# Exponentials four pieces nearer to their maxima, maxima handed over by halves, and distance transforms one quarter later in an eight-batch attention and feed-forward kernel

## The reference

```python
x = x + attn_a(ln(x))   # values V = ln(x) wv; positions pos = ln(x) w3d + b3d, 3 per token
                        # dist = sqrt(sum((pos_i - pos_j)^2)); attn = softmax(-dist/4, causal); attn V wo + bo
x = x + ffn(ln(x))      # sigmoid(xr Wr) * (relu(xk Wk)^2 Wv), with xr, xk mixed from a token and the one before
x = x + attn_b(ln(x))   # 16 heads of 16: softmax(q k / 4, causal) v
x = x + ffn(ln(x))
```

## Time and profile before

| | |
|---|---|
| median of 3 runs | 2104.01 us (2102.3 to 2108.9) |
| profiled execution, device time | 2109.85 us |
| its span, first to last instruction | 2108.1 us |
| mean granted TensorE clock | 0.943 |
| busy: PE, DVE, ACT, POOL | 1849.2, 1467.0, 1323.7, 728.2 us |

### The profile page before, as it was taken

One profiled execution on the slowest core, in us unless ns is written; L12 is line 12 of the kernel. 1 busy time (PEld: TensorE's weight loads), 2 busy tenths in 40 slices (PEclk: granted clock), 3 DMA queues, 4 the chain that ended last, 5 costly groups with the idle time before them and its releaser, 6 DMA issues. The chain is left out here.

```text
span 2108.1 us, 32379 instructions
## 1 busy us (share of the span) xinstructions
PE 1849.2 (88%) x9842; PEld 922.5 (44%) x9842; DVE 1467.0 (70%) x4288; ACT 1323.7 (63%) x2585; POOL 728.2 (35%) x879
## 2 busy tenths in 40 slices
PE   5677898889997999889998899979998899988986
PEld 4453443335543455434543355434544345322423
DVE  5576778767676677667786667766776677768642
ACT  3564355876569565776758665695657766455664
POOL 1342332234333253333443243333532334312313
PEclk8797899999998999999999899989999999989998
DMA  3006113111131112410132111311124101322000
GB/s 85 1 23 123 26 56 67 31 31 32 55 76 31 31 31 82 80 21 12 41 110 42 31 31 56 76 31 31 34 83 76 22 11 41 99 33 50 13 21 20
DMA packets 64346, 97.26 MB, mean 46 GB/s; under 512 B 15655, under 2 KB 58029, under 8 KB 58030
## 3 DMA queue, kind: packets, MB, share of 16 engines
q1 hardware_dynamic: 64174, 95.20, 20.2%
HBM read 61.09 MB, written 33.55 MB: 45 GB/s over the span
## 5 line engine op out<-in xcount | busy, mean ns | idle before, releaser
L973 ACT ACTIVATE pt<-exp_bank 128x512 f32<-128x512 f32 (+1 forms) x1216 | 698.9, 582 | 526.6 <-PE exp_bank L935 521.0
L989 DVE CUSTOM_DVE_ANT_0 max_bank<-max_bank,mask 128x128 f32<-128x128 f32 (+3 forms) x1024 | 501.8, 500 | 400.9 <-PE max_bank L922 386.4
L922 PE MATMUL max_bank<-ks,qs 96*128 96x512 bf16 (+3 forms) x1536 | 523.5, 346 | 85.9 <-DVE piece_max L992 44.9
L935 PE MATMUL exp_bank<-qs,ks 98*128 98x512 bf16 (+3 forms) x1536 | 515.4, 342 | 40.0 <-ACT pt L973 37.0
L992 DVE TENSOR_REDUCE piece_max<-max_bank 128x1 f32<-128x512 f32 x512 | 344.1, 686 | 94.4 <-PE max_bank L922 90.2
L954 PE MATMUL o_bank<-pt,v 128*17 128x512 f32 (+3 forms) x3072 | 334.1, 508 | 13.7 <-POOL pt L1011 11.0
L922 PEld LDWEIGHTS max_bank<-ks,qs 96*128 96x128 bf16 x1536 | 150.9, 99 | 399.5 <-DVE piece_max L989 140.9
L1011 POOL TENSOR_SCALAR_AFFINE_SELECT pt<-pt 128x512 f32<-128x512 f32 x256 | 171.5, 670 | 412.6 <-ACT pt L973 411.8
L935 PEld LDWEIGHTS exp_bank<-qs,ks 98*128 98x128 bf16 x1536 | 152.4, 100 | 236.0 <-ACT pt L973 118.5
L633 PE MATMUL side<-vp,p 128*128 128x260 f32 x576 | 171.4, 423 | 28.7 <-ACT p L560 21.0
L412 ACT ACTIVATE xh<-xs,shift,rstd 128x256 f32<-128x256 f32 x256 | 149.7, 596 | 47.8 <-POOL shift L401 47.8
(11 more groups left out here) (119 smaller groups left out, 2348.4 us busy)
## 6 DMA issues: line engine op xcount, KB each, us to landing
parts_dram<-parts SPq DMA_DIRECT2D x64, 384.0 KB, 2.6
qs<-parts_dram SPq DMA_DIRECT2D x192, 128.0 KB, 7.2
ks<-parts_dram SPq DMA_DIRECT2D x32, 384.0 KB, 4.7
xs<-in_L_attn_a_x_dram SPq DMA_DIRECT2D x16, 512.0 KB, 4.2
ks<-parts_dram SPq DMA_DIRECT2D x32, 256.0 KB, 5.4
out_dram<-xs SPq DMA_DIRECT2D x16, 512.0 KB, 3.1
ks<-parts_dram SPq DMA_DIRECT2D x32, 128.0 KB, 5.8
qs<-neg_maxT SPq DMA_DIRECT2D x64, 8.0 KB, 1.9
```

Source lines behind the costliest of these rows:

```text
L922: pe.matmul(max_bank[u % MAX_BANKS][:, 0:k1 - k0], qs[r][0:KROWS, j, P * tile:P * (tile + 1)], ks[r][0:KROWS, j, k0:k1], start=True, stop= ...
L935: mm = pe.matmul(exp_bank[k % EXP_BANKS][:, (q1 - q0) * slot:(q1 - q0) * (slot + 1)], ks[r][:, j, P * kt:P * (kt + 1)], qs[r][:, j, q0:q1] ...
L973: act.activation(pt[:, e % 2, j + 1 - heads:j + 1, 0:w], exp_bank[k % EXP_BANKS][:, 0:heads * w].rearrange("p (j n) -> p j n", j=heads), A ...
L989: dve.tensor_tensor_reduce(scores, scores, mask[:, HALF - w:HALF], 1.0, LOWEST, ALU.add, ALU.max, piece_max[:, j, m:m + 1]).then_inc(max_f ...
```

## The change

- `LEAD` goes from 14 to 10: the exponential product in a quarter belongs to the piece ten before the maxima piece. Outputs and the last batch's `ffn4` move with it.
- The maxima are handed over by halves: the first after the group's fourth piece, the second after its twelfth. Each half has its own two small DVE operations, two turns on PE and a copy; SP sends it with eight transfers (two parts, four heads) of 1 KB, each from four rows of `neg_maxT` into a piece of one row of `qs`. PE waits for the first half at the group's first exponential product and for the second at that of its fifth piece.
- In `att1`, ACT's Ln, root and Exp, POOL's selects and PE's products come one quarter later. In batch 0 ACT's two squares of a piece come in its first two quarters. In batch 1 the third square moves from DVE to ACT.
- The rows of ones are filled by POOL, early in the setup (behind its second layer-norm shift), instead of by DVE.

```diff
-LEAD = NP + 2
+LEAD = NP - TPH + 2
...
-        "attend": [("attend", t, PIECE_AT[attended_from(t)] + 2, t // 2 + 1, 1, 2) for t in range(NT)],
+        "attend": [("attend", t, PIECE_AT[attended_from(t)] + 3, t // 2 + 1, 1, 2) for t in range(NT)],
...
-    rows = [(4 * NP * (g + 1) + 1, ("maxima", g)) for g in range(GROUPS)]
+    rows = [(4 * (NP * g + (NP if h else TPH)) + 1, ("maxima", g, h)) for g in range(GROUPS) for h in range(2)]
...
             for p in range(NP + 1):
+                for k in range(2 if n == 0 and p < NP else 0):
+                    yield at(PIECE_AT[p] + k)
+                    square(p, k)
                 for k in range(3):
-                    if p < NP and (k < 2 or n > 1):
+                    if p < NP and n > 0:
                         yield at(PIECE_AT[p] + PIECE_TIME[p] * 2 * k // 6)
                         square(p, k)
                     if p > 0:
-                        yield at(PIECE_AT[p] + PIECE_TIME[p] * (2 * k + 1) // 6)
+                        yield at(PIECE_AT[p] + PIECE_TIME[p] * (2 * k + 1) // 6 + 1)
                         transform(p - 1, k)
...
                 if p >= 2 and DIAGONAL[p - 2]:
-                    yield at(PIECE_AT[p])
+                    yield at(PIECE_AT[p] + 1)
                     select(p - 2)
...
-                    pe.wait_ge(crow_ready, 32 * (g + 1))
+                    pe.wait_ge(crow_ready, 256 * g + 128)
+                if m == TPH and j == 0:
+                    pe.wait_ge(crow_ready, 256 * g + 256)
...
-                if m == NP - 1 and j == GH - 1:
+                if m in (TPH - 1, NP - 1) and j == GH - 1:
+                    h = 0 if m < TPH else 1
+                    half = piece_max[:, :, TPH * h:TPH * (h + 1)]
                     dve.wait_ge(max_free, u + 1)
...
+                    if h == 1:
+                        dve.tensor_tensor(half, half, piece_max[:, :, NT:NP], ALU.max).then_inc(c_step, 1)
+                        dve.wait_ge(c_step, 3 * g + 2)
+                    dve.tensor_scalar(neg_max[:, h, 0, :, :], half, -1.0, None, ALU.mult).then_inc(c_step, 1)
+                    dve.wait_ge(c_step, 3 * g + 1 + 2 * h)
+                    dve.scalar_tensor_tensor(out=neg_max[:, h, 1, :, :], in0=half, scalar=-1.0,
+                                             in1=neg_max[:, h, 0, :, :], op0=ALU.mult,
                                              op1=ALU.subtract).then_inc(negmax_ready, 1)
...
-        def sp_maxima(g):
-            yield EMPTIED_AT["maxima", g] + 1
+        def sp_maxima(g, h):
+            yield EMPTIED_AT["maxima", g, h] + 1
             r = g % STACKS
-            nc.sync.wait_ge(negmaxT_ready, g + 1)
+            nc.sync.wait_ge(negmaxT_ready, 2 * g + h + 1)
             for c in range(2):
-                nc.sync.dma_start(qs[r][KROWS + c:KROWS + c + 1, :, :], neg_maxT[:, c, :]
-                                  ).then_inc(crow_ready, 16)
+                for j in range(GH):
+                    nc.sync.dma_start(qs[r][KROWS + c:KROWS + c + 1, j, HALF * h:HALF * (h + 1)],
+                                      neg_maxT[TPH * j:TPH * (j + 1), h, c, :]).then_inc(crow_ready, 16)
...
-            for r in range(STACKS):
-                yield SETUP_AT[7] + 12 + 8 * r
-                dve.memset(ks[r][KROWS:SROWS, :, :], 1.0).then_inc(rows_of_ones, 1)
...
             pool = nc.gpsimd
             yield SETUP_AT[6] + 6
+            pool.wait_ge(shift_ready, 2)
+            for r in range(STACKS):
+                pool.memset(ks[r][KROWS:SROWS, :, :], 1.0).then_inc(rows_of_ones, 1)
+            pool.wait_ge(rows_of_ones, STACKS)
             pool.memset(vp[:, :, ONE:ONE + 1], 1.0).then_inc(consts_ready, 1)
...
-                body = {"att1": [dve_att1(at, n)] + ([dve_squares(at, n)] if n < 2 else []), "proj3": [dve_proj3(at, n), dve_values3(at, n)]}.get(s, []) if h == 0 else []
+                body = {"att1": [dve_att1(at, n)] + ([dve_squares(at, n)] if n == 0 else []), "proj3": [dve_proj3(at, n), dve_values3(at, n)]}.get(s, []) if h == 0 else []
```

More of the change, by code:

```diff
@@ L273, in bass_hybrid @@
         piece_max = sb("piece_max", [P, GH, NP])
-        neg_max = sb("neg_max", [P, 2, GH, NT], BF16)
-        neg_maxT = sb("neg_maxT", [GH * NT, 2, P], BF16)
+        neg_max = sb("neg_max", [P, 2, 2, GH, TPH], BF16)
+        neg_maxT = sb("neg_maxT", [GH * TPH, 2, 2, P], BF16)
         pt = sb("pt", [P, 2, GH, HALF])
@@ L984, in dve_att3 @@
                 if m == 0 and j == 0 and g > 0:
-                    dve.wait_ge(negmax_ready, g)
+                    dve.wait_ge(negmax_ready, 2 * g)
                 scores = max_bank[u % MAX_BANKS][:, 0:w]
@@ L1024, in sp_att3, with pe_maxima @@
                         sp_load(n + X_BUFFERS, h)
[L1027 to L1030, removed]
+        def pe_maxima(g, h):
+            yield PARTS_AT["maxima", g, h][0]
+            nc.tensor.wait_ge(negmax_ready, 2 * g + h + 1)
+            bank = side_job(("maxima", g, h), negmaxT_ready, 2 * g + h + 1)[:, :].bitcast(BF16)
             for c in range(2):
-                mm = nc.tensor.transpose(bank[0:GH * NT, P * c:P * (c + 1)],
-                                         neg_max[:, c, :, :].rearrange("p j t -> p (j t)"), identb[:, :])
+                mm = nc.tensor.transpose(bank[0:GH * TPH, P * c:P * (c + 1)],
+                                         neg_max[:, h, c, :, :].rearrange("p j t -> p (j t)"), identb[:, :])
@@ L1034, in pe_maxima, with dve_maxima @@
             mm.then_inc(negmaxT_full, 1)
-        def dve_maxima(g):
-            yield EMPTIED_AT["maxima", g]
-            nc.vector.wait_ge(negmaxT_full, g + 1)
+        def dve_maxima(g, h):
+            yield EMPTIED_AT["maxima", g, h]
+            nc.vector.wait_ge(negmaxT_full, 2 * g + h + 1)
             if g > 0:
[L1040 to L1043, removed]
+                nc.vector.wait_ge(crow_ready, 256 * (g - 1) + 128 * (h + 1))
+            bank = side_of("maxima", g, h)[:, :].bitcast(BF16)
+            nc.vector.tensor_copy(neg_maxT[:, h, :, :],
+                                  bank[0:GH * TPH, 0:2 * P].rearrange("p (c n) -> p c n", c=2)
@@ L1207, in schedule @@
         def schedule(setup, attention, maxima, output, stage):
-            parts = list(setup) + [maxima(g) for g in range(GROUPS) if maxima]
+            parts = list(setup) + [maxima(g, h) for g in range(GROUPS) for h in range(2) if maxima]
             parts += [output(g, h) for g in range(GROUPS) for h in range(2) if output]
```

## The result

The kernel after takes 2166.0 us (median of 4 runs, 2162.0 to 2168.0), the kernel before 2106.5 (median of 4, 2102.3 to 2110.0): a ratio of 1.028, interval 1.0254 to 1.0308. It is 2.8% slower, where 2092 was forecast and the range ended at 2118. The profiled execution of after has a span of 2164.9 us against 2108.1, so +56.8 to explain.

What follows compares the result with a forecast made beforehand. PE was taken to bound most of a batch, ACT the stretch with distance work, DVE or the bank hand-over where no side job is due. Terms summed to -12.4 us: 2097.5 profiled, 2092 on the median's scale; range 2070 to 2118.

Steps and rivals of the forecast that it cites:

- sixteen small transfers a group: Maxima hand-over through SP: steady groups covered, seven short groups 0.9 to 2.5 us late; +12, up to about +41.
- the time left is as before: Second half's hand-over: still eight quarters after the group's end; copy to first exponential 6.17 us steady, 2.81 at shortest.
- The end: Last group: its first four exponential pieces run beside the last maxima, so everything after comes earlier; -9.9 us.
- Front start of exps: First group: four pieces of exponentials move into maxima pieces 10 to 13, where PE is busy; +4 (0 to +7).
- New partners: Across groups: wide exponentials fall beside wide maxima, saving time without side jobs and where PE idles; -16 (0 to -30).
- Rival 2: No change overall: new partners gain nothing and half maxima cost what they cost; 2108 us, chance 0.15.
- Maxima by halves: Every group: extra turns on PE, a copy and small operations on DVE, hidden where ACT limits; +17 (0 to +35).
- Ones on POOL: Front: without DVE's three fills, ACT's waits for distances shrink, less delay to DVE's copies; -5.5 (0 to -9.5).
- rival 4: Setup: each fill on POOL holds DVE's copies until it ends, so the front gains nothing; 2097 us, chance 0.08.
- Squares: First two batches' distances: earlier squares on ACT -3, third square moved from DVE to ACT -3; together -6 us.
- A quarter later: Attention's logs, roots, exps, selects and products: ACT waits less, and so PE behind POOL; -8 (-20 to +5).
- Rival 1: Maxima transfers: an issue step of 0.75 us makes short and most steady groups late; 2121 us, chance 0.17.

Runs made afterwards that it cites:

- b1_after_four: The kernel after with each half's maxima sent by four transfers of both rows instead of eight; 2110.7 us, ratio 1.0030.
- b2_halves_four: The kernel before with only the maxima by halves and distance 10, four transfers a half; 2109.4 us, ratio 1.0034.
- c2_eight_second: The kernel after with four transfers for the first half's maxima, eight kept for the second; 2165.4 us, ratio 1.0327.
- a1_halves: The kernel before with only the maxima by halves, distance 10 and eight transfers a half; 2142.1 us, ratio 1.023.
- f1_before_lead13: The kernel before with exponentials 13 pieces behind instead of 14, maxima whole, two transfers a group; 2187.2 us, ratio 1.0407.
- c3_lead12_four: The kernel before with only the maxima by halves, four transfers a half, exponentials 12 pieces behind; 2157.1 us, ratio 1.0298.
- e1: The kernel after with distance 11 instead of 10, eight transfers a half kept; 2101.5 us, ratio 0.9964.
- e2: The kernel after with distance 11 and four transfers a half; 2097.9 us, ratio 0.9973.
- d1_lead14_four: The kernel before with only the maxima by halves, four transfers a half, exponentials still 14 pieces behind; 2117.8 us, ratio 1.0090.
- a3_ones: The kernel before with only the three fills of ones moved from DVE to POOL; 2112.2 us, ratio 1.0043.
- a4_squares: The kernel before with only the squares changed: first batch's two earlier on ACT, second batch's third on ACT; 2113.2 us, ratio 1.0040.
- b4_no_quarter: The kernel after without the quarter's delay of logs, roots, exps, selects and products; 2143.8 us, ratio 1.0188.
- a2_quarter: The kernel before with only logs, roots, exps, selects and their products a quarter later; 2115.0 us, ratio 1.0103.
- e3: The kernel before with maxima by halves, distance 11, four transfers a half and the changed squares; 2088.5 us, ratio 0.9905.

## Why the prediction was wrong, step by step

**The failed step is the sixteen small transfers a group, +12 (up to +41), and in them "the time left is as before".** Their real price was 53 us (the kernel after against b1_after_four). That PE would wait at the second half was right; the issue step and the room were mis-sized, the parts' stores behind the issues and the price of a wait beyond its own length were put at nothing.

- *The issue.* 0.62 us a step, not 0.45. The row of three-row transfers (0.39) was the wrong neighbour; the median of the maxima's own (0.59) was the right one, which the rival had as the argument against itself. Time needed from the end of the copy: 5.97 us with eight transfers, 3.69 with four. This alone would not have put the forecast wrong: with 0.62 in the prediction's own sum the seven short groups are 7 x 1.19 us later and the six with a room of 6.17 us are 0.37 late, so the term is +23 and the forecast 2103.
- *The room.* The prediction took the shortest room of the kernel before's steady groups, 6.17 us from the copy's start, and kept it. But the room changed, and most in other groups. The exponentials of groups 7, 11, 15, 19 and 23 had 7.4 to 7.7 us in the kernel before. At a distance of 10 (b2_halves_four, where nothing waits there) they have 5.0 to 6.1, as other pieces stand between. With the quarter's delay as well (b1_after_four) they have 4.7 to 4.9. Group 19 in the three, copy and first product that uses it:

```profile
1372.81 0.27 DVE L1042 COPY neg_maxT<-side 32x256 bf16<-32x256 bf16 x1
...
1380.52 0.63 PE L935 MATMUL exp_bank<-qs,ks 98*128 98x512 bf16 x1
```

```profile
1384.92 0.21 DVE L1044 COPY neg_maxT<-side 32x128 bf16<-32x128 bf16 x1
...
1391.03 0.63 PE L937 MATMUL exp_bank<-qs,ks 98*128 98x512 bf16 x1
```

```profile
1389.50 0.21 DVE L1047 COPY neg_maxT<-side 32x128 bf16<-32x128 bf16 x1
...
1394.19 0.63 PE L940 MATMUL exp_bank<-qs,ks 98*128 98x512 bf16 x1
```

  Hence waits of 1.1 to 1.6 us before the exponentials of just these groups in the kernel after (they run beside the next group's maxima, so in the windows these waits stand in groups 8, 12, 16, 20 and 24), 9.4 us in all with groups 5, 9 and 25, and 18.8 in eight short groups in place of 14.5 in seven. The prediction priced the delay and the transfers apart; beside each other they cost more.
- *The queue behind the issues.* The prediction had "the batch's stores and part stores keep their places" and no price for it. Their place is behind the eight issues (5.2 us with gaps at group 14, where the two transfers of the kernel before took 1.5), DVE waits for the store, and 14.3 us of the 51.8 between c2_eight_second and b1_after_four stand in the groups where it does.
- *The price of a wait.* This was missing. Between c2_eight_second and b1_after_four, with equal instruction counts on every engine, the waits of PE differ by 27.1 us and the span by 51.8: PE's busy time is 23.2 us longer (1875.5 against 1852.3). The mean granted clock is 0.933 against 0.945: (1 - 0.933) x 2164.2 = 145 us of full clock not granted against (1 - 0.945) x 2112.4 = 116, 29 more. Without the groups where DVE waits, 37.5 us of span came with 27.1 of waits, 1.4 for one; between a1_halves and b2_halves_four it is 17.1 / 16.2 = 1.1, in f1_before_lead13 against the kernel before 75.6 / 53.7 = 1.4, and from group 28 on 20.1 / 12.1 = 1.7. That the waits bring the clock down is argued from the two coming together, from group 28 on above all, and not shown by itself: the clock also falls where nothing waits (mean 0.930 in c3_lead12_four; 0.87 and 0.90 in groups 3 and 4 of b2_halves_four, 1.00 in both in the kernel before).

The Trainium skill's advice to coalesce small transfers (DMA: Bandwidth & Descriptors, Rules for kernel authors), which the prediction set against this part and then priced low, was the right one: halving their number took 53 us off the kernel after. It was worth that much because the room was short: at a distance of 11 the same sixteen cost nothing that can be measured (e1 against e2: 2101.5 and 2097.9 us, ratios 0.9964 and 0.9973).

The other terms:

- *The end, -9.9:* right as a mechanism, -7.8 in b1_after_four. In the kernel after 3.3 us of wait and a clock of 0.75 took all but 1.3 of it.
- *Front start of exps, +4:* group 0 is 1.9 us longer in the kernel after, 3.3 in a1_halves. Right.
- *New partners, -16:* failed. The distances 14 and 10 with four transfers take 1356.1 and 1354.4 us in groups 5 to 26. Rival 2's first half was true. The gain was to be had at 11 (-22 against 10), which was found by trying it and not by this argument, and 12 costs +34. The like-with-like argument of the earlier trace rows fits 11 against 12, but does not rank 14; side jobs fall on other pieces with each distance, and what each share is stays open.
- *Maxima by halves, +17:* right in number, not in place, so in part luck. d1_lead14_four, which has the halves and neither long issues nor new partners, has a ratio of 1.009, that is 19 us. But a price of 0.55 a group makes 12 us in groups 5 to 26, and there its profile has 1.4 more than the kernel before (1356.1 against 1354.7); of 11.1 us in all 4.7 stand in groups 0 to 4.
- *Ones on POOL, -5.5:* failed by rival 4. a3_ones gives +1 to +17. The prediction had the rule of the Trainium skill (SBUF — State Buffer, Who interferes with whom) as a rival at 0.08, for want of a row of a fill; this trace now has it, four DVE operations held for 2.2 to 3.6 us. The rival's reckoning came true: the squares start 8.0 us late in a3_ones, and the three fills that no longer stand among the distances give just that back by the twelfth piece.
- *Squares, -6:* near in the front (group 0 begins 4.3 us earlier in a4_squares, and 1.5 in b4_no_quarter, which has the ones on POOL too), unclear at the end: ratio 1.004 alone, 2093.0 to 2088.5 us at a distance of 11, measured on two chips.
- *A quarter later, -8:* failed. a2_quarter loses 1.03%. PE's wait for POOL shrank as expected, but the time ahead of group 5 grew by 9.3 us (453.4 against 444.1), 7.0 of them in group 4 at the lower clock. Beside late transfers the delay cost about 20 us (b4_no_quarter), where it also took up to 1.4 us of the room and raised PE's waits for the maxima from 17.7 to 28.2 us.

Of what was to show it: the fills ended before 37 us and the waits of L550 in 30 to 60 us are down from 10.3 to 1.9, both as written, and yet the front gained nothing: the start had moved, and the delay held the rest. The eight issues take 4.9 us and not 3.2 to 3.6. The two signs of being wrong both came: waits in steady groups, and batches 1.1 to 6.1 us longer from group 8 to 24 (group 8 to 12 takes 248.9 us in place of 245.9).

Rival 1 came true in kind, but its price (2121) and its threshold (0.68 us a step) were both wrong. By the prediction's own rows the groups with a room of 6.17 us are late from (6.17 - 0.30 - 1.9) / 7 = 0.57 on; 0.62 was enough, the more as the room became smaller. And the loss of 59.5 us was more than three times the 17 by which 2121 lies above the 2104 before.

## What to carry to other kernels

When a hand-over is moved, measure the room in the new order and not in the old one: the pieces that lie between release and use change with the distance, a delay that looks unrelated takes from the same room, and one piece more (11 for 10) was worth 64 us here. Count a wait of PE at more than its length: here the span grew by 1.1 to 1.7 us for each microsecond of it, mostly at a lower granted clock. And look at what stands behind the new issues in the queue, not only at what waits for them. Price transfer issues by the nearest row of the same queue with its gap, and try each distance and each part alone, since the delay and the ones on POOL, small beside the main edit, cost 9.5 us between them at the best distance (e2 against e3, medians).

## What the runs showed of the hardware

- The kernel before, unchanged, took from 2081.6 to 2124.6 us over all its runs, and its span goes with the mean granted clock: 2083.3 us at 0.956, 2095.7 at 0.949, 2108.8 at 0.942 on one chip. So a ratio near 1 needs many runs of both kernels.
- In these traces the clock is granted at one of two levels, 1.2 or 2.4 GHz, and nearly the same work in another order can get another mix of them: group 4 has a mean of 1.00 in the kernel before and of 0.82 in a2_quarter, with 237 and 234 products.
- A transfer of four rows (1 KB) takes SP 0.573 us to issue and one of eight rows (2 KB) 0.61; SP's time for 16 or 8 a group is thus nearly proportional to their number.
